# Attention row maxima split into three bf16 parts before the transpose instead of after it

## The reference, cut to what matters

```python
q = jnp.einsum('bse,oe->bso', x, wq) + bq
qh = q.reshape(HEADS, b, s, hd)          # 16 heads of 8; keys and values are the same tensor
scores = jnp.einsum('hbqd,hbkd->hbqk', qh, qh) * scale
attn = jax.nn.softmax(scores, axis=-1)
out = jnp.einsum('hbqk,hbkd->hbqd', attn, qh)
```

## Time and profile before

| what | value |
|---|---|
| median of three runs | 2725.08 us (2714.4 to 2730.01) |
| the profiled execution, its own time | 2714.58 us |
| its span | 2712.8 us |
| TensorE (PE) busy | 2122.5 us, 78% |
| DVE busy | 1472.9 us, 54% |
| ACT busy | 1233.0 us, 45% |
| mean granted clock of TensorE | 0.892 of full |

### The profile page before, as it was taken

How to read it: one execution, slowest core, us unless ns; L and a number is a source line. 1 busy time by engine, 2 the same in 40 slices (tenths; PEclk the granted TensorE clock), 3 DMA queues, 4 the chain that set the end, 5 groups by cost and what they waited for, 6 DMA issues and landing times.

```text
span 2712.8 us, 42689 instructions
## 1 busy us (share of the span) xinstructions
PE 2122.5 (78%) x13612; PEld 1580.5 (58%) x13612; DVE 1472.9 (54%) x4206; ACT 1233.0 (45%) x2621; POOL 645.1 (24%) x656
## 2 busy tenths in 40 slices
PE   3667572488768788998898789879988998778875
PEld 2445351366546556775686467647765775655754
DVE  5887434553465674566556565556565356346512
ACT  4766313443335445544644464445454445334421
POOL 3111003222130133123222322232233133022042
PEclk9877895699889889999999899999998999888987
DMA  7000000011211212311131113221321312311111
GB/s 234 25 0 0 1 1 0 25 35 49 61 47 39 67 46 59 80 50 52 51 87 52 44 49 87 55 59 41 79 63 53 83 54 55 81 32 52 38 56 45
DMA packets 228960, 141.40 MB, mean 52 GB/s; under 512 B 116489, under 2 KB 206732, under 8 KB 228754
## 3 DMA queue, kind: packets, MB, share of 16 engines
q1 hardware_dynamic: 174320, 85.60, 12.7%
q0 software_dynamic: 16960, 34.74, 4.5%
q10 hardware_dynamic: 37474, 18.46, 2.3%
HBM read 82.48 MB, written 57.16 MB: 51 GB/s over the span
## 4 chain that ended last, share of the span: by engine, by line
PE 51%; DVE 17%; issue 15%; ACT 9%; DMA 2%; POOL 2%; SPq 2%; another core or an unknown queue 1%; DVEq 0%; ACTq 0%; POOLq 0%
PE PS L898 14%; PE PS L866 9%; PE PS L1191 4%; PE PS L1177 4%; PE PS L1154 4%; PE PS L1172 3%; PE PS L1366 2%; DVE small L327 2%; DVE AR L1076 2%; ACT AR L1127 2%; ACT AR L827 1%; PE PS L901 1%; DVE xnT L1253 1%; PE PS L857 1%
## 5 line engine op out<-in xcount | busy, mean ns | idle before, releaser
L898 PE MATMUL PS<-AR,W 128*128 128x256 f32 x2560 | 639.7, 397 | 20.0 <-DVE AR L785 17.1
L785 DVE TENSOR_TENSOR AR<-AR,PS 128x512 f32<-128x512 f32 (+1 forms) x384 | 228.6, 597 | 666.3 <-ACT AR L827 516.3
L898 PEld LDWEIGHTS PS<-AR,W 128*128 128x128 f32 x2560 | 487.0, 199 | 90.9 <-DVE AR L785 14.0
L1127 ACT ACTIVATE AR<-PS 128x512 f32<-128x512 f32 x512 | 304.2, 599 | 376.4 <-PE PS L1177 322.3
L827 ACT ACTIVATE AR<-PS 128x512 f32<-128x512 f32 (+1 forms) x384 | 201.0, 525 | 583.6 <-PE PS L898 422.4
L1076 DVE TENSOR_REDUCE AR<-PS 128x2 f32<-128x512 f32 x512 | 339.0, 688 | 214.7 <-PE PS L1154 180.3
L866 PE MATMUL PS<-AR,WO 128*128 128x256 f32 (+1 forms) x1536 | 385.4, 393 | 0.0
L866 PEld LDWEIGHTS PS<-AR,WO 128*128 128x128 f32 (+1 forms) x1536 | 286.8, 194 | 79.8 <-issue 42.5
L1154 PE MATMUL PS<-AR 128*128 128x256 bf16 x1024 | 211.4, 295 | 55.0 <-DVE AR L1076 27.7
L1172 PE MATMUL PS<-AR 128*128 128x256 bf16 x1024 | 212.8, 292 | 52.7 <-ACT AR L1127 33.4
L1177 PE MATMUL PS<-AR,pick 96*128 96x256 bf16 x1024 | 212.3, 291 | 26.9 <-DVE AR L1089 26.6
(11 more groups left out here) (354 smaller groups left out, 2815.7 us busy)
## 6 DMA issues: line engine op xcount, KB each, us to landing
AR<-XE SPq DMA_DIRECT2D x128, 128.0 KB
YE<-AR ACTq DMA_DIRECT2D x128, 128.0 KB
AR<-QD SPq DMA_DIRECT2D x384, 32.0 KB
QD<-AR SPq DMA_DIRECT2D x8, 768.0 KB, 5.4
AR<-KD SPq DMA_DIRECT2D x64, 96.0 KB
W<-in_L_ffn_w_kernel_dram SPq DMA_DIRECT2D x2, 2560.0 KB, 13.4
OD<-AR SPq DMA_DIRECT2D x128, 36.0 KB
X<-in_L_attn_dense_dram SPq DMA_DIRECT2D x8, 512.0 KB, 4.2
```

The lines of the kernel that those rows point to most:

```text
L785: ins = dve.tensor_tensor(hf[:, cols], gl[i % 2][:, cols], H[:, 2 * (i % 2) + 1, cols], ALU.mult)
L898: mm = pe.matmul(H[:, b0, b * CAP:(b + 1) * CAP], w0[:, e, hb * P:(hb + 1) * P], xeT[e % 2], start=True, stop=True)
L1127: act.activation(EX[:, li, :], H[:, 2 + i % 2, :], ACT.Exp, scale=A_SCALE).then_inc(S["a_ex"], 1)
```

## The change: where the maxima are split, and by whom they are copied

DVE splits `mx` (128 partitions x 16 columns, SBUF) with four linked instructions into `MS`, a bf16 tile with three blocks of 16 columns (the rest zeros). TensorE transposes all 128 columns of `MS` as bf16, and now waits for the split (`a_ms`) in place of the reductions. ACT copies 48 rows of the result to `MP` and signals `a_mp`. `pick` has 48 rows in place of 96. The split stands at li = 3 of the DVE's slots in place of li = 6; the transpose stays at li = 5; the copy stands behind the exponential of li = 5. For the first piece of a group the split takes the place of `parts` in the lists, so it stays at slot 20 of m0, as does the transpose; the copy stands at slot 21.

```diff
-MROWS = 96
+MROWS = 3 * 2 * PB
-        mrest, mmid = ar.take((P,)), ar.take((P,), BF16)
+        mrest = ar.take((2 * PB,))
+        MS = [ar.take((P // (2 * PB), 2 * PB), BF16) for _ in range(2)]
...
+        def turned_maxima(c):
+            return side_bank(c).bitcast(BF16)[:, 0:P]
...
-                if b == 0 and c >= 2:
-                    dve.wait_ge(S["a_mxT"], NPC * n + c - 1)
...
-            def parts(c):
-                dve.wait_ge(S["a_mxT"], NPC * n + c + 1)
+            def split(c):
+                dve.wait_ge(S["a_mx"], PB * (NPC * n + c + 1))
                 if c >= 2:
-                    dve.wait_ge(S["a_slot"], PB * (NPC * n + c - 1))
-                mt, hi = side_bank(c)[0:R, :], MP[c % 2][0:R, :]
-                ch.link(dve.tensor_scalar(hi, mt, -1.0, None, ALU.mult))
-                ch.link(dve.scalar_tensor_tensor(mrest[0:R, :], mt, -1.0, hi, ALU.mult, ALU.subtract))
-                ch.step(dve.tensor_copy(MP[c % 2][32:32 + R, :], mrest[0:R, :]))
-                ch.link(dve.tensor_copy(mmid[0:R, :], mrest[0:R, :]))
-                dve.tensor_tensor(MP[c % 2][64:64 + R, :], mrest[0:R, :], mmid[0:R, :],
-                                  ALU.subtract).then_inc(S["a_mp"], 1)
+                    dve.wait_ge(S["a_mxT"], NPC * n + c - 1)
+                m, parts = mx[c % 2].rearrange("p a b -> p (a b)"), MS[c % 2]
+                ch.link(dve.tensor_scalar(parts[:, 0, :], m, -1.0, None, ALU.mult))
+                ch.link(dve.scalar_tensor_tensor(mrest, m, -1.0, parts[:, 0, :], ALU.mult, ALU.subtract))
+                ch.link(dve.tensor_copy(parts[:, 1, :], mrest))
+                dve.tensor_tensor(parts[:, 2, :], mrest, parts[:, 1, :], ALU.subtract).then_inc(S["a_ms"], 1)
...
-                return [lambda b=b: maxima(0, b) for b in range(PB)] + [lambda: parts(0), lambda: values(0)]
+                return [lambda b=b: maxima(0, b) for b in range(PB)] + [lambda: split(0), lambda: values(0)]
...
-                    if li == 6:
-                        parts(c + 1)
+                    if li == 3:
+                        split(c + 1)
...
+            def turned(c):
+                act.wait_ge(S["a_mxT"], NPC * n + c + 1)
+                act.copy(MP[c % 2][0:MROWS, :], turned_maxima(c)[0:MROWS, :]).then_inc(S["a_mp"], 1)
...
+                if li == 5 and c + 1 < NPC:
+                    turned(c + 1)
...
             def maxima(c):
-                pe.wait_ge(S["a_mx"], PB * (NPC * n + c + 1))
+                pe.wait_ge(S["a_ms"], NPC * n + c + 1)
                 if c >= 1:
                     pe.wait_ge(S["a_va"], NPC * n + c + 1)
-                pe.transpose(side_bank(c)[0:2 * PB, :], mx[c % 2].rearrange("p a b -> p (a b)"),
-                             ident[:, :]).then_inc(S["a_mxT"], 1)
+                pe.transpose(turned_maxima(c), MS[c % 2].rearrange("p a b -> p (a b)"),
+                             identb[:, :]).then_inc(S["a_mxT"], 1)
...
+                if R.has(-1) and R.i != NG and not opening(R):
+                    b.put((FIRST_SCORES[PB] + 1, attend_act(act, R.g(-1), None)))
```

More of the change, by code:

```diff
@@ L934, in experts_sp @@
                     load_xe(sp, p, n, e, k + e, w)
-        A_CH = 2 + NPC * 4
+        A_CH = 2 + NPC * 3
         NS = NC * CB
@@ L1056, in side_bank @@
             return Y[:, 1, 0:P] if c == 0 else PS[:, 0, 0:P]
+        def turned_maxima(c):
+            return side_bank(c).bitcast(BF16)[:, 0:P]
         def attend_dve(dve, n, ch, beside):
-            R = 2 * PB
             def values(c):
@@ L1119, in out @@
                          sum_bank(r)).then_inc(S["a_osb"], 1)
+            def turned(c):
+                act.wait_ge(S["a_mxT"], NPC * n + c + 1)
+                act.copy(MP[c % 2][0:MROWS, :], turned_maxima(c)[0:MROWS, :]).then_inc(S["a_mp"], 1)
+            if beside is None:
+                return lambda: turned(0)
             for i in range(NS):
@@ L1917, in one @@
                 n = R.g(-1) if R.has(-1) else None
-                ch = None if n is None else Chain(dve, S["a_ch"], n * A_CH + 6)
+                ch = None if n is None else Chain(dve, S["a_ch"], n * A_CH + 5)
                 b = Beside()
@@ L1975, in one @@
                 if n is not None:
-                    assert ch.k == A_CH - 6
+                    assert ch.k == A_CH - 5
                 N = R.after()
@@ L2033, in fill @@
                     b.put(*zip((9, 10, 10, 11, 11, 12, 12), [*la, *ta]),
-                          (13, lambda: hold(act, S["m_scatter0"], 512)), (13, fa[0]), (13, fa[1]))
+                          (13, lambda: hold(act, S["m_scatter0"], 512)), (13, fa[0]), (13, fa[1]),
+                          (SOON_SCORES[PB], attend_act(act, 0, None)))
                 return b
@@ L2046, in one @@
                 n = R.g(-1) if R.has(-1) else None
+                if opening(R):
+                    b.put((0, attend_act(act, n, None)))
                 attend_act(act, n, b, LEAD + 16 * E * R.run(EXPERTS, "m1"))
@@ L2068, in one @@
                     b.put(*zip(at[1:], [*la[1:], *ta, *fa]))
+                if turned_last(R):
+                    b.put((LAST_SCORES[PB] + 1, attend_act(act, g, None)))
                 if R.has(2):
@@ L2210, in rest @@
                     ch.link(pool.memset(VA[k][:, :, :, AD:AD + 1], 1.0))
-                    ch.link(pool.memset(MP[k], 0.0))
+                    ch.link(pool.memset(MS[k], 0.0))
                 assert ch.k == ONES
@@ L2411, in _ @@
             ch.wait()
-            ch.step(pool.tensor_tensor(pick[0:MROWS, :], identb[0:MROWS, 0:2 * PB], identb[0:MROWS, 32:32 + 2 * PB],
+            ch.step(pool.tensor_tensor(pick[0:MROWS, :], identb[0:MROWS, 0:2 * PB], identb[0:MROWS, 2 * PB:4 * PB],
                                        ALU.add))
@@ L2415, in _ @@
                                        ALU.add))
-            ch.step(pool.tensor_tensor(pick[0:MROWS, :], pick[0:MROWS, :], identb[0:MROWS, 64:64 + 2 * PB], ALU.add))
+            ch.step(pool.tensor_tensor(pick[0:MROWS, :], pick[0:MROWS, :], identb[0:MROWS, 4 * PB:6 * PB], ALU.add))
             ch.link(pool.tensor_tensor(join[0:3 * AD, :], join[0:3 * AD, :], identb[0:3 * AD, 2 * AD:3 * AD],
```

## The result

The changed kernel takes 2791.23 us (median of 4 runs, 2779.18 to 2800.29), the kernel before 2724.34 (4 runs, 2714.4 to 2730.01): a ratio of 1.0225, interval 1.0179 to 1.0271. That is 66.9 us slower, against a forecast of 15.1 slower and a range that ended at 2759. The profiled execution took 2800.29 us, 85.7 more than that of before; its span is 2798.5.

The account below looks back on a forecast made before the run. TensorE bounds the experts; in the attention TensorE and DVE wait for each other by turns. Pauses +22.9, clock +9.5 and attention with the transpose saving -17.3 sum to +15.1 us: 2740.2 against 2725.08 us, range 2719 to 2759.

Parts of the forecast that it names:

- part 1: DVE chain 1.40 to 0.77 us, ACT's 0.27 us copy at no cost, fewer rows nothing, transpose -3 us.
- The saving of 3 us on the transpose: The bf16 transpose saves between 0 and 0.11 us of TensorE's queue; half taken, -3 us over 64.
- Part 2: Slot 20 before groups 2 to 6: TensorE pauses 4.2 us five times, +21.1; before group 7, +2.5; total 22.9 us.
- part 3: TensorE's clock at half after each of the five long pauses, 1.9 us each: +9.5 us, bounds 0 and 12.
- -0.7 for groups 0 and 1: First pieces of groups 0 and 1: the chain, serial already, gets shorter, -0.7 us for both.
- Part 4: Inside the attention: of 37.7 us of L1177 waits 14.3 come back; with part 1's 3 us, -17.3, between -8 and -35.
- slots 40 to 48: Attention pieces where DVE is the bound, six groups: L1177's wait gives 0.65 to 0.8 in place of 1.2 to 1.5.
- the routing's being late: In the attention, routing behind the split is late by up to 0.77 us in six pieces: 1.8 us less gain.
- The wait at slot 37: In the attention the transpose waits 2.4 us for the split, hidden where DVE is the bound, not in group 6.
- rival D: The wait at the transpose is not hidden: +30 to +35 us, 2755 to 2760 us; chance 0.18.
- C: DVE bounds more of the attention, some -45 us there, and the clock stays up: -17, 2708 us; chance 0.10.
- A: The forecast itself: slot 20's pauses and the clock outweigh the attention, +7 to +24 us; chance 0.50.

Follow-up runs that it names:

- before48: The kernel before with only MROWS = 48 in place of 96, which leaves out the third bf16 part of the maxima; 2698.32 us, ratio 1.0221 to the kernel before.
- rows96: The changed kernel with MROWS = 96 in place of 48, the upper 48 rows zeros; 2633.88 us, ratio 0.9992 to the kernel before.
- after_b: The changed kernel run again without edit, on the chip of the kernel before's rerun; 2703.91 us, ratio 1.0247 to the kernel before.
- rows64: The changed kernel with MROWS = 64 in place of 48; 2687.92 us, ratio 1.0203 to the kernel before.
- rows72: The changed kernel with MROWS = 72 in place of 48; 2632.18 us, ratio 0.9981 to the kernel before.
- join128: The changed kernel with 96 rows, the first piece's split at slot 18, and the value step's contraction widened from 24 to 128 rows with zeros; 2593.24 us, ratio 0.9830.
- rows96_early: The changed kernel with 96 selector rows and the first piece's split right behind its last reduction; 2598.11 us, ratio 0.9849 to the kernel before.
- late: The changed kernel with 96 rows, the first piece's split at slot 18, and interior transposes and copies at li = 6, not 5; 2605.1 us, ratio 0.9884.
- late_join128: The changed kernel with 96 rows, first split at slot 18, transposes and copies at li = 6, value contraction of 128 rows; 2591.8 us, ratio 0.9825.
- the early split: The changed kernel with the first piece's split right behind its last reduction, slot 18 in place of 20; alone with 48 rows 2665.75 us, ratio 1.0095.
- before_b: The kernel before run again without edit, for its trace on the later chip; 2641.0 us, ratio 1.0013.
- pad: The changed kernel with 96 rows, first split at slot 18, and a useless DVE reduction at li = 6 in 56 pieces; 2610.45 us, ratio 0.9908.

## Why the prediction was wrong, step by step

**The failed step** is the sentence of part 1: "Rows of `MP` and `pick`: the columns streamed stay 256, nothing." It priced the matmul by the columns that it streams and didn't ask what stands before it. Slots alternate loads of 128 rows with loads of 48, and each change from one to the other leaves 0.2 us in which no weights are loaded, ahead of L1184 and again behind it, in all 512 slots. By before48 it costs 61.8 us alone, by rows96 against after_b 0.0255 of 2637, 67 us. The timelines put a bound on the idle times: a slot gets 0.22 us longer, 512 x 0.22 = 113 us. It is less because where the slot waits for DVE or ACT the idle time lies beside that wait, and what is measured may hold 9 to 45 us of lower clock besides (the estimate beside the table above). It is a term of about the whole error: 66.9 measured less 15.1 forecast is 51.8, and what the other terms were off by goes the other way.

The row that should have warned stood in the trace before. The value step has a load of 24 rows between loads of 128. Timeline of group 6, before:

```profile
2236.39 0.21 PEld L1177 LDWEIGHTS PS<-AR,pick 96*128 96x128 bf16 x2
2236.81 0.61 PEld L1139 LDWEIGHTS PS<-join,AR 24*128 24x128 bf16 x16 [0.21 <-issue]
```

A load of 96 rows follows one of 128 with no bracket; the load of 24 rows has one of 0.21. A nearer row, of 48 rows, stood in the same trace and in the very stretch of the earlier trace rows, the second product of an expert:

```profile
1183.59 0.29 PEld L866 LDWEIGHTS PS<-AR,WO 48*128 48x128 f32 x2 [0.33 <-issue]
...
1184.22 1.59 PEld L898 LDWEIGHTS PS<-AR,W 128*128 128x128 f32 x8 [0.33 <-issue]
```

and, from the waits of the kernel before:

```profile
PEld PS L866 <- issue: 42.5, 128, 0.3
```

All 128 pairs of 48 rows have 0.33 us ahead of them and some 0.33 or more behind. (Their fp32 matmuls take 0.38 us each, so 0.33 isn't the number for bf16.) With 0.2 at each end of the new kind of load these rows bounded the cost beforehand: 1024 x 0.2 = 205 us at most, nothing at least. The Trainium skill ("TensorEngine Tiling (Array Packing)", "Key Properties") says that a change of the tiling mode, not merely of the tile, drains the engine, and its "Tiling Modes" list row modes of 32, 64 and 128. If the row count alone picks the smallest mode that holds it, which neither section says, a matmul of 48 or 64 rows next to ones of 128 is a change of mode, and one of 72 or 96 isn't; the border in rows64 and rows72 agrees with that, and so does the idle time that join128 removes. It spoke against this change, and the prediction should have weighed it as a rival. The idle time isn't the same behind every change: the values' 24 rows, with matmuls of 8 columns, are followed by a load of 128 rows after 0.02 us (2163.00 to 2163.02 in rows96_early), so the 0.2 us go with the matmuls of 256 columns that the load stands behind. And it isn't only a matter of more or less than 64 rows: in the changed kernel the values' 24 rows (L1146) stand right behind the 48 of L1184 in 56 places and have the same 0.21 us ahead of them in all 56, as the list of modes has it. That each load really changes a mode, and that the 0.2 us are a drain, is the reading that fits; the records show only that no load begins and that TensorE's next matmul starts later.

**The other part of part 1** held. The four instructions take 0.17 us each and 0.80 together (1744.14 to 1744.94), forecast 0.77. ACT's copy takes 0.25, forecast 0.27, and costs nothing that shows: the selector's loads never wait for it with the transpose at li = 5, only in late and late_join128 (7.9 us each). The saving of 3 us on the transpose can't be seen.

**Part 2, the first piece of a group, and part 3, the clock,** held in place and in size. Forecast 22.9 us for five pauses of 4.2 and one of 2.5, plus 9.5 for the clock; read 4.20 to 4.38 of idle loads and 3.96 to 4.14 of idle matmuls, one of 2.5, with the clock at half for some 3.4 us at each (5 us at 0.66), which loses 1.7 where 1.9 was taken. Without its -0.7 for groups 0 and 1, part 2 with the clock is 33.1; the early split, which takes both away, is worth 35.8 us with 96 rows and 38 to 40 with 48. One prop of part 3 is thinner than it says: the earlier trace rows show one pause and two stretches at half clock.

**Part 4, the attention,** was right in sign and less than half in size. Forecast -17.3, bounds -8 and -35; rows96_early, which has next to nothing else left, measures -38.4, and the stage sums say -41 and -45. It went wrong above all at slots 40 to 48, at whose end I kept at most 0.8 us of a wait. The window of that piece in group 4 (from one first L1177 or L1185 of a piece to the next), before_b:

```profile
1753.42:1766.07 12.65, 11.06 (x97) 6.83 (x97) 10.22 (x37) 5.21 (x10) 3.88 (x4) 0.79 0.06 19
```

rows96_early:

```profile
1722.62:1732.57 9.95, 8.97 (x98) 6.33 (x97) 8.91 (x35) 5.36 (x11) 4.48 (x5) 0.96 0.09 29
```

12.65 against 9.95 us, 2.7 won, with 1.31 less work on DVE and the clock at 0.96 in place of 0.79. Over all eight groups this piece sums to 97.5 us in before_b and 77.6 in rows96_early: 19.9 of the 41. Part of it is the whole wait at its end, and that hung on the place of the split. Timeline at that end, DVE and the load in before_b, then DVE in rows96_early:

```profile
1763.26 1.28 DVE L1076 TENSOR_REDUCE AR<-PS 128x2 f32<-128x512 f32 x2
1764.45 0.27 DVE L1085 TENSOR_SCALAR AR<-PS 16x128 bf16<-16x128 f32 x1
...
1766.07 0.11 PEld L1177 LDWEIGHTS PS<-AR,pick 96*128 96x128 bf16 x2 [1.71 <-DVE AR L1089]
```

```profile
1727.54 0.17 DVE L1085 TENSOR_SCALAR AR<-AR 128x16 bf16<-128x16 f32 x1
...
1728.24 0.28 DVE L633 TENSOR_TENSOR AR<-PS,small 128x128 f32<-128x128 f32 x1
```

The old split stood behind two reductions that themselves had stood behind the routing, and the next piece waited 1.71 us for it; the new one is issued ahead of the routing (L633 and on), and the next piece's first load waits for nothing. I had counted the new order only as the routing's being late. The shorter chain is a small part: in pad, with DVE's work given back, this piece sums to 81.6 us, 4.0 more than in rows96_early. The clock may be a large one: before_b spent 44.5 of its 97.5 us at half clock, rows96_early 3.8 of 77.6, and half of that difference, 20 us, is an upper estimate of what the clock gave back. Order and clock weren't separated; fewer pauses and a higher clock came together.

The wait at slot 37 is there, and by its size it is the best single reading of the forecast: 2.4 us were predicted, and rows96_early shows

```profile
1717.13 0.10 PEld L1171 LDWEIGHTS PS<-identb,AR 128*128 128x128 bf16 x1 [2.42 <-DVE AR L1088]
```

Whether it is hidden is the question of rival D. Late speaks for hidden: moving the transpose takes most of the wait away (27.3 to 6.2 us) and wins nothing, though part of that is the copy's new wait.

**The rivals.** C ("DVE is the bound of more of the attention than I think", a gain of some 45 us) is the one that described the inside of the attention: its -45 and its clock that stays up stand against -41 to -45 measured and 28 to 52 us less at half clock, where the forecast had -17.3; but pad shows that less than half of it is the shorter chain, on which C rested. Its total was far off, since the rows were in it at nothing too. D's total came nearest to the truth, by luck: late speaks against its mechanism, and the 48 rows were not in it. What made the kernel slower than A was in no rival.

**The sum as it now stands**, on one chip: rows 62 to 68, pauses and clock 36 to 40, attention -38: 60 to 70 us. Measured 67.2 (2703.91 less 2636.71), and 66.9 in the first measurement. This agreement is no proof by itself, for most of the terms are differences between the same kernels and add up by the way they are made; the term that stands on its own is before48's 61.8.

## What to carry to other kernels

Price a matmul by its neighbours too: fewer rows in the contraction saved nothing here (a load of 48, 72 or 96 rows takes 0.10 us), and 64 or fewer between matmuls of 128 rows and 256 columns left 0.2 us without a load at every change and made the slot 0.22 us longer, so pad with zeros to more than 64 (rows96, rows72, join128). Look for such brackets in the trace of the kernel before: they stood there, on a load of 48 rows. When a producer moves ahead of a transpose, look at each place where the transpose used to run free of that producer, above all a hand-made first piece under other work, and put the producer right behind its inputs there. And test a bundle of edits one by one: here two lines turn a loss of 2.5% into a gain of 1.5%, and none of the change's own idea had to be given up.

## What the runs showed that was not expected

- The border of the idle time between 64 rows (ratio 1.0203) and 72 rows (0.9981), and its size of 0.19 to 0.21 us in both directions, behind bf16 matmuls of 256 columns.
- The clock stays at half through whole pieces of the attention in which TensorE is recorded as busy throughout: 23.7 us at 0.50 in the changed kernel's group 4. That attention took 104.6 us in the first measurement's trace and 92.6 in after_b, so how often this happens differs between executions; what sets it off was not tried. With 48 or 64 selector rows the attentions had more half clock than with 96 or 72 in every pair of traces.
- The same kernel took 2724.34 us in the first measurement and 2636.71 later, 3.2% less, with almost the same ratio of the changed kernel (1.0225 and 1.0247). The attentions hold nearly all of it: 761.5 and 694.3 us of spans of 2712.8 and 2640.4, with 158 and 96 us of them at half clock. The chip of the first measurement isn't known, so whether it is the chip is open.
